# GpSimd makes layer A's mask and query latents earlier, VectorE adds eps and evicts early products ahead of its weight chunks

## The reference

```
layer A:  x += tanh(g) * xattn_A(LN(x), LN(context), mask)   8 heads of 64; kv = context and gated latents
          x += tanh(g) * moe(LN(x))                          8 experts, top 2 per token, width 512
layer B:  x += tanh(g) * xattn_B(LN(x), LN(context), mask)   16 heads of 64
          x += tanh(g) * ffn_B(LN(x))                        rows and weights quantised, 256 -> 1024,
                                                             depthwise conv of 3, activation, 1024 -> 256
LN(v) = (v - mean) * rsqrt(var + 1e-5) * gamma + beta
xattn: softmax(q k^T + mask) v, then an output projection; keys are 112 latents and 375 context rows
```

## Time and profile before

| | |
|---|---|
| median of 3 runs | 1506.27 us (1496.41 to 1508.53) |
| profiled execution | 1507.64 us, its span 1505.9 us |
| granted TensorE clock, mean | 0.935 |
| busy: TensorE, VectorE, ScalarE, GpSimd | 83%, 71%, 65%, 74% of the span |
| DMA engines | 239.94 MB, mean 159 GB/s |

### The profile page before, as it was taken

How to read it: one execution, slowest core, us unless ns; L and a number is a source line. 1 busy time by engine, 2 the same in 40 slices (tenths; PEclk the granted TensorE clock), 3 DMA queues, 4 the chain that set the end, 5 groups by cost and what they waited for, 6 DMA issues and landing times.

```text
span 1505.9 us, 44898 instructions
## 1 busy us (share of the span) xinstructions
PE 1252.2 (83%) x16822; PEld 980.5 (65%) x16822; DVE 1075.0 (71%) x2786; ACT 973.2 (65%) x2319; POOL 1116.6 (74%) x1359
## 2 busy tenths in 40 slices
PE   1868787768769898977999999899999999999842
PEld 0545565547658776655887887677777777777631
DVE  4868786876555556775666766688888888888744
ACT  2868785555545576654655555687888887787731
POOL 5869787686566675547676777789889888988754
PEclk9989998889999999987999999999999999999965
DMA  7499999886999974547999999544655455454520
GB/s 223 98 232 229 230 241 221 166 219 148 242 179 249 235 171 91 93 101 181 236 229 252 247 256 241 107 106 97 104 97 105 104 108 104 95 110 102 78 41 6
DMA packets 439336, 239.94 MB, mean 159 GB/s; under 512 B 388960, under 2 KB 420560, under 8 KB 430544
## 3 DMA queue, kind: packets, MB, share of 16 engines
q1 hardware_dynamic: 407496, 172.87, 56.6%
q10 hardware_dynamic: 28552, 56.86, 12.4%
q0 software_dynamic: 3072, 7.34, 1.8%
HBM read 107.78 MB, written 35.50 MB: 95 GB/s over the span
## 4 chain that ended last, share of the span: by engine, by line
PE 32%; POOL 23%; DMA 13%; DVE 10%; issue 7%; ACT 6%; SPq 4%; DVEq 2%; ACTq 1%; POOLq 0%
PE bank_ring L1089 6%; DMA probs_turned<-probs 6%; POOL probs L651 6%; DMA expert_up<-experts_up 6%; PE bank_ring L1075 5%; PE bank_ring L1127 5%; PE bank_scores L1049 4%; PE bank_out L1108 3%; POOL raw_weights L696 3%; PE bank_x L1188 2%; ACT scores L852 2%; PE bank_x L1141 2%; POOL raw_weights L697 2%; POOL affine L627 2%; SPq L521 2%
## 5 line engine op out<-in xcount | busy, mean ns | idle before, releaser
L651 POOL TENSOR_TENSOR probs<-scores,probs 112x487 f16<-112x487 f32 x384 | 425.9, 1126 | 223.1 <-ACT probs L859 218.3
L852 ACT ACTIVATE scores<-scores,score_min 112x487 f32<-112x487 f32 x384 | 265.5, 693 | 81.8 <-DVE score_min L1340 79.5
L1340 DVE CUSTOM_DVE_ANT_0 scores<-bank_scores,mask 112x487 f32<-112x487 f32 x384 | 239.1, 660 | 48.9 <-PE bank_scores L1049 43.8
L859 ACT ACTIVATE probs<-scores 112x487 f16<-112x487 f32 x384 | 214.7, 604 | 37.0 <-DMA probs_turned<-probs 21.8
L1089 PE MATMUL bank_ring<-weights,kv_B 128*128 128x128 f16 x3072 | 196.8, 222 | 1.8 <-DVE keys L1352 1.8
L1089 PEld LDWEIGHTS bank_ring<-weights,kv_B 128*128 128x128 f16 x3072 | 185.8, 99 | 11.1 <-DVE keys L1352 2.5
L1108 PE MATMUL bank_out<-values,probs_turned 128*128 128x64 f16 x4608 | 171.3, 194 | 23.3 <-DMA probs_turned<-probs 22.7
L1357 DVE SCALAR_TENSOR_TENSOR values<-bank_ring,values 128x512 f16<-128x512 f32 x192 | 131.2, 683 | 80.4 <-ACT values L879 80.4
L879 ACT ACTIVATE values<-bank_ring 128x512 f16<-128x512 f32 x192 | 112.6, 587 | 110.5 <-PE bank_out L1108 109.1
L1075 PE MATMUL bank_ring<-kv_B,weights 128*128 128x488 f16 x768 | 181.1, 372 | 0.0
L1108 PEld LDWEIGHTS bank_out<-values,probs_turned 128*128 128x128 f16 x4608 | 158.6, 99 | 26.7 <-DMA probs_turned<-probs 13.0
(11 more groups left out here) (230 smaller groups left out, 2474.8 us busy)
## 6 DMA issues: line engine op xcount, KB each, us to landing
expert_up<-experts_up SPq DMA_DIRECT2D x43, 1024.0 KB, 5.3
expert_down<-experts_down SPq DMA_DIRECT2D x43, 512.0 KB, 6.8
raw_weights<-in_weights ACTq DMA_DIRECT2D x8, 1536.0 KB, 11.1
experts_up<-expert_up ACTq DMA_DIRECT2D x8, 1024.0 KB, 4.8
raw_weights<-in_weights ACTq DMA_DIRECT2D x6, 1024.0 KB, 8.3
probs_turned<-probs SPq DMA_TRANSPOSE x384, 3.3
context_turned_B<-kv_B ACTq DMA_DIRECT2D x16, 375.0 KB, 9.1
kv_B<-context_turned_B ACTq DMA_DIRECT2D x16, 375.0 KB, 3.7
```

The lines of the kernel that those rows point to most:

```text
L651: pool.tensor_tensor(PR[:, u % 4, 1, 0:KEYS], S[:, u % 4, 0:KEYS], PR[:, u % 4, 0, 0:KEYS], ALU.subtract).then_inc(probs_split, 1)
L852: act_e.activation(S[:, u % 4, 0:KEYS], S[:, u % 4, 0:KEYS], ACT.Exp, bias=rmin[:, u % 4:u % 4 + 1], scale=-1.0, accum_out=rsum[:, g % 2, ...
L859: act_e.activation(PR[:, u % 4, 0, 0:KEYS], S[:, u % 4, 0:KEYS], ACT.Copy).then_inc(probs_ready, 1)
L1340: dve.tensor_tensor_reduce(out=S[:, u % 4, 0:KEYS], in0=bS[u % 2][0:TOK, 0:KEYS], in1=mask[:, m, 0:KEYS], scale=1.0, scalar=3.0e38, op0=AL ...
```

## The change

Five edits:

1. GpSimd's `split_latents` is cut in three. `split_query_latents(n)` runs at step 4n-5, after that step's split_context of layer B and ahead of its split_probs. `make_mask(0, n)` runs at step 4n-4, ahead of split_context. What is left at step 4n-3 is the gated latents alone, and they raise `kv_ready`. Sequence 0 keeps one block in step -5, in the new order. Layer B's `split_latents` still makes its mask.
2. ScalarE's `round_latents` is cut likewise: the query latents' high part at step 4n-5, ahead of `round_context`; the gated ones stay at step 4n-4.
3. SP loads layer A's mask bytes at step 4n-6 instead of 4n-5, waiting for `mask_made` instead of `kv_ready`.
4. The multiplication and addition of eps in `rstd` move to VectorE: a drain and one `tensor_scalar` after each `bn_aggr`, two for P. GpSimd keeps the power.
5. On VectorE the early evictions (and `gate_hidden`) stand ahead of `split_expert` and `quantise_ffn_weights`. `split_l1_chunk` stays ahead of `gate_hidden` in steps with an expert tile, and comes after the evictions in others.

```diff
             def load_mask(layer, n):
-                sp.wait_ge(kv_ready[layer if n else 0], n if n or not layer else NSEQ)
+                if layer == 0:
+                    sp.wait_ge(mask_made, n)
+                else:
+                    sp.wait_ge(kv_ready[layer if n else 0], n if n else NSEQ)
...
-                if (j - 3) % 4 == 0 and 0 < (j + 5) // 4 < NSEQ:
-                    load_mask(0, (j + 5) // 4)
+                if (j - 2) % 4 == 0 and 0 < (j + 6) // 4 < NSEQ:
+                    load_mask(0, (j + 6) // 4)
...
             def rstd(stage, n, cols):
-                m, r = mv[stage], rs[stage]
+                r = rs[stage]
                 pool.wait_ge(stats_ready[stage], n + 1)
-                after(pool.tensor_tensor(r[:, 0:cols], m[:, 0:cols, 1], growth[:, 0:cols], ALU.mult))
-                after(pool.tensor_tensor(r[:, 0:cols], r[:, 0:cols], bias[:, 0:cols], ALU.add))
                 pool.tensor_tensor(r[:, 0:cols], r[:, 0:cols], minus_half[:, 0:cols], ALU.pow)\
                     .then_inc(rstd_ready[stage], 1)
...
+            def split_query_latents(n):
+                pool.wait_ge(x1_drained, X1_AT[("p_lat", n)])
+                for kb in range(KB):
+                    scale, shift = latent_vec(V_GLAT, kb)
+                    last = pool.tensor_scalar(affl[:, 0, kb], latT[:, kb], scale, shift, ALU.mult, ALU.add)
                 after(last)
+                pool.wait_ge(latq_hi, n + 1)
+                after(pool.tensor_tensor(latq[:, n % 2, :, 1], affl[:, 0], latq[:, n % 2, :, 0], ALU.subtract))
+
+            def make_mask(layer, n):
                 a, b = (MASKED, 0.0) if layer == 0 else (-MASKED, MASKED)
...
+                return pool.tensor_scalar(mask[:, n % 2, TOK:KEYS], mask8[:], a, b, ALU.mult, ALU.add)
+
+            def split_latents(layer, n):
+                c = 8 + V_GLAT if layer else V_GATED
...
+                pool.wait_ge(lat_hi[layer], n + 1)
+                last = pool.tensor_tensor(lo, affl[:, 0], hi, ALU.subtract)
+                if layer:
+                    after(last)
+                    last = make_mask(layer, n)
+                last.then_inc(kv_ready[layer], 1)
+                if layer == 0:
+                    pool.wait_ge(kv_ready[0], n + 1)
...
                 if (j + 4) % 4 == 0 and 0 < (j + 4) // 4 < NSEQ:
+                    make_mask(0, (j + 4) // 4).then_inc(mask_made, 1)
                     split_context((j + 4) // 4, 0, 0)
...
+                if (j + 5) % 4 == 0 and 0 < (j + 5) // 4 < NSEQ:
+                    split_query_latents((j + 5) // 4)
...
                 if (j + 5) % 4 == 0 and 0 <= (j + 5) // 4 < NSEQ:
-                    round_context((j + 5) // 4)
+                    n = (j + 5) // 4
+                    round_latents(n, latq[:, n % 2], V_GLAT, latq_hi)
+                    round_context(n)
                 if (j + 4) % 4 == 0 and 0 <= (j + 4) // 4 < NSEQ:
-                    round_latents((j + 4) // 4)
+                    n = (j + 4) // 4
+                    round_latents(n, kv[0][:, n % 2, :, :, 0:TOK], V_GATED, lat_hi[0])
...
                 dve.drain()
-                dve.bn_aggr(mv[stage][0:TOK, 0, :], bn[0:TOK, at, :]).then_inc(stats_ready[stage], 1)
+                dve.bn_aggr(mv[stage][0:TOK, 0, :], bn[0:TOK, at, :])
+                dve.drain()
+                dve.tensor_scalar(rs[stage][0:TOK, 0:1], mv[stage][0:TOK, 0, 1:2], 1.0 + LN_EPS, LN_EPS * LN_EPS,
+                                  ALU.mult, ALU.add).then_inc(stats_ready[stage], 1)
...
+                if m[0]:
+                    for c in l1_chunk(j - 1):
+                        split_l1_chunk(c)
+                    gate_hidden(m[0][1], m[0][2], m[0][3])
+                for t in early(j):
+                    part(t)
                 for c in expert_chunks(j - 1):
                     split_expert(c)
                 quantise_ffn_weights(j)
-                for c in l1_chunk(j - 1):
-                    split_l1_chunk(c)
-                if m[0]:
-                    gate_hidden(m[0][1], m[0][2], m[0][3])
-                for t in early(j):
-                    part(t)
+                if not m[0]:
+                    for c in l1_chunk(j - 1):
+                        split_l1_chunk(c)
```

56 lines of the change are left out of this document (24 added, 32 removed).

## The result

The changed kernel takes 1534.68 us, the median of four runs (1526.26 to 1536.71), against 1506.47 before: ratio 1.0221, 95% interval 1.0169 to 1.0273. It is 28 us slower. A run over 1.5% above its kernel's fastest is left out of every ratio in this text. The profiled execution took 1536.71 us, its span 1535.0, 29.1 more than before's.

A forecast was written before the change was run, and what follows sets the result against it. No engine was taken to bound the whole: the chain lies on TensorE 32%, GpSimd 23%, DMA 13%. Terms -0.3 -1.2 -6.5 +1.7 -4 +1.5 -3.5 -1 sum to -13.3: 1493 us against 1506.3, range 1472 to 1511.

The forecast's parts named there:

- one added wait is within 0.1: GpSimd's run ahead of a sequence's first query product: 2.0 of 3.6 us leave, and the added wait costs within 0.1.
- The slower rival: Query latents ahead of split_probs delay transposes 1.6 to 2.2 us, behind bursts, 11 us more each: 1526 us, chance 12%.
- Step 2: TensorE's 3.6 us wait for GpSimd's mask at the first query product shrinks: -1.2 us, bounds 0 and 2.0.
- A wait removed just ahead of such a stretch is only paid later: 65 to 268 us: a 14.74 us transpose follows; three of six mask waits count as followed by one, three as free.
- 65 to 268 us: Layer A: -3.3 us from six waits for GpSimd's mask and -3.2 from VectorE's early evictions, together -6.5.
- The scatter: Around 341 us: the last scatter, behind more GpSimd work, delays the first expert product: +1.7 us, bounds 0 and 2.2.
- 380 to 554 us: TensorE's 26.0 us of waits for expert_up shrink as SP issues these loads sooner: -4 us, bounds 0 and 9.
- eps: Less GpSimd work in rstd, more on VectorE: layer B -3.5 us, tail -1, start -0.3, layer A +1.5.
- VectorE's order: 65 to 268 us: early products evicted ahead of weight chunks, some keys 1.28 us late: -3.2 us, between -6 and +6.
- the third stretch above: 780 to 955 us: TensorE busy 166.68 of 175 us, DMA share 1.01 at 239 GB/s; the change can do nothing.
- The last sign named: Forecast wrong if probabilities' transposes newly queue behind bursts, or DMA share falls well below 0.98 while both stretches shrink 20 us.

The follow-up runs named there:

- queries_behind_probs: The changed kernel with GpSimd's query latents of step 4n-5 behind both split_probs of that step instead of ahead of them: ratio 1.0139 to the kernel before.
- rounding_ahead: The changed kernel with ScalarE's rounding of the query latents ahead of its rounding of the probabilities in step 4n-5, not at the step's end: ratio 1.0100.
- act_round_early: The kernel before with only ScalarE's rounding of the query latents moved a step earlier, GpSimd and SP keeping their order: ratio 1.0084.
- after_l1_late: The changed kernel with ScalarE's first load of layer B's raw weights, 1 MB, at step 39 instead of 37: ratio 1.0165 to the kernel before.
- the main pair: The kernel before, 1506.47 us, and the changed kernel with all five edits, 1534.68 us: ratio 1.0221.
- the light pair: The kernel before and the changed kernel, each with five sixths of the experts' raw loads left out: 1488.9 us (0.9916) and 1512.1 us (1.0103).
- eps_only: The kernel before with only the multiplication and addition of eps moved to VectorE: ratio 1.0055.
- order_only: The kernel before with only VectorE's early evictions moved ahead of its weight chunks: ratio 0.9980.
- no_latents: The changed kernel without the moves of mask, query latents and mask load, so only eps on VectorE and VectorE's new order: ratio 1.0003.
- spread_l1_late: The kernel before with experts' raw loads in three smaller DMAs each and layer B's first raw-weight load at step 39 instead of 37: ratio 0.9935.
- mask_early: The kernel before with the mask made at step 4n-4 on GpSimd and its bytes loaded at 4n-6 on SP, all latents staying: ratio 1.0011.

## Why the prediction was wrong

*The step that failed* is in the part on GpSimd: "one added wait is within 0.1". The handshake was priced, not the place of its partner. The prediction knew that GpSimd would wait for ScalarE ("ahead of its exponentials, and GpSimd waits for these"), but the rounding stands at the end of its step, ahead of the next step's exponentials and behind both roundings of the probabilities of its own. The waits were 94.7 us in 15 times, 6.3 each, 47.6 us more in all than GpSimd waited for ScalarE before, and behind each are queued two split_probs, two transposes on SP and ScalarE's rounding four heads on, which needs the buffer. Without the wait the loss is 0.8 to 1.2% smaller (queries_behind_probs, rounding_ahead). Nothing in the trace of before showed this wait, but both orders did. A second term was left out, as if it cost nothing: ScalarE's rounding a step earlier, which alone costs 0.8% (act_round_early); why it does stays open.

*The slower rival* had the family right: query latents ahead of split_probs, transposes issued late and behind bursts, 1526 us. It was priced by 1.6 to 2.2 us of work per sequence, which rounding_ahead shows not to be the main part, and given 12%. In step 7 the delay was 5.75 us. So it was near the result, 1534.7, partly by luck. Its 11 us for each transpose were taken against a median of 3.3 us over the whole run, and from 50 to 300 us the median before is 6.3. The range was also narrower than the chances: it ended at 1511 with 8% above, while this rival at 1526 had 12%.

*Step 2* (-1.2): the wait at the query product fell from 3.6 to 2.0 us, but behind it came one of 6.7 us for a transpose:

```profile
PE bank_out L1123 <- DMA probs_turned<-probs: 6.7, 1, 6.7
PE bank_x L1077 <- POOL kv_A L643: 2.0, 1, 2.0
```

The transpose at 50.84 was 0.5 us ahead of the spill and took 11.5 us; before it was 1.25 ahead and landed in 6.1. The step took 4.1 us more. "A wait removed just ahead of such a stretch is only paid later" held here, with interest. How much is chance: in the profile of after_l1_late, the same program up to step 36, this wait is 2.7 us.

*65 to 268 us* (-6.5) measured plus 18. Its parts were near: the waits for GpSimd fell by 11.1 of at most 12, those for VectorE's evictions by 3.5 of at most 6, and five keys were to come late by 1.28; they did so six times, 6.1 us. What was missing in this profile is 11.7 us more for transposes and 6.3 us more of busy TensorE. The forecast let the DMAs absorb no more than the gain; they can take more. In the profile of after_l1_late the wait for transposes in these steps is only 20.1 us, and the stretch is still 10.9 us longer than before's.

*The scatter* (+1.7) was right where it was priced: the first expert product starts 16.2 us after the step's start before (325.5 to 341.75) and 17.9 after (353.1 to 371.04). Its wait is 6.62 us, for which "some 10" was expected. The step is 3.9 us longer, since behind it TensorE waits 1.9 us for the keys. What was not seen is the jump that lies beside it, some 6 or some 10 us from scatter to load; in both profiles of the main pair it is the long one, in the light pair it is 5 of the 11.2 us that the changed kernel loses in the step.

*380 to 554 us* (-4) gave nothing: TensorE waits 28.8 us in twelve times (380 to 632) where it waited 26.0 in five (350 to 600), and some 20 were expected.

```profile
PE bank_ring L1142 <- DMA expert_up<-experts_up: 28.8, 12, 8.9
```

Steps 43 and 47 are 1.9 and 5.0 us shorter, steps 51, 53 and 55 together 3.9 longer. What was not seen is step 59, 3.2 us longer: VectorE waits 8.46 us there for the gathered rows of the mixture's result, and TensorE 9.1 us for VectorE's queries behind them (before 7.00 and 6.6).

*eps.* Layer B: forecast -3.5 (2.7 to 5.0 less). TensorE's waits from 985 to 1469 us (for the earlier trace rows):

```profile
PE bank_x L1249 <- DVE raw_weights L1601: 7.9, 9, 1.1
PE bank_x L1253 <- DVE raw_weights L1610: 6.0, 10, 0.6
```

Nine waits of 0.9 us and the second group up, as forecast, and it is edit 4 that does it: the first group is 7.8 us in eps_only and stays 12.7 in order_only. The two groups together are 2.8 us less. But the time hardly shows it: from step 104 to 191 the changed kernel takes 492.3 us, eps_only 492.5 and order_only, without eps, 492.8, against 493.0 before, and all profiles lie between 491.4 and 494.0. Of the 6 us that come back after step 60, 5 lie between steps 60 and 104, 3.6 of them from step 80, about the stretch of which the prediction said that the change can do nothing; from 60 to 104 order_only gains 3.7, no_latents 2.0, eps_only 1.9. In layer A +1.5 was too little: eps_only as a whole is 0.55% slower, some 8 us, and its one profile, at 1503.9 us of span, doesn't show where. That stays open.

*VectorE's order* (-3.2) has the size of order_only's 0.998, or 3 us, but that is luck as far as the runs tell: the interval reaches from 8 us faster to 2 slower, and in the stretch for which it was forecast order_only's profile is 10.4 us longer (208.6 against 198.2 from step 5 to 31). The Trainium skill's figure, 341 GB/s for transfers of 1 MB ("DMA: Bandwidth & Descriptors", Bandwidth), was weighed against rows and left; the third stretch above again shows only 242 GB/s at share 0.98.

*The last sign named*, that the forecast is wrong "if the probabilities' transposes queue behind bursts where they didn't", is what the trace of the changed kernel shows in step 2, and the wait for turned probabilities grew past 18.7 us, to 30.4.

## What to carry to other kernels

When an instruction moves ahead on one engine, look up where its partner stands in the other engine's order, not only what the handshake costs: a producer at the end of the same step turned a 0.6 us subtraction into a 6 us stall for everything queued behind. Put such a consumer behind the step's critical hand-overs, or the producer ahead of them. And where stretches run with full DMA queues, an issue that slips past another engine's burst can change price in a jump (from 6 to 10 us here), so look at the order of issue between queues, not only at microseconds. Last, take a second profile of the same program before a single step is explained: here one step took 8.6 us in one and 16.2 in the other.

## What the runs showed of the hardware

- TensorE's busy time for the same products varies with the granted clock, and not with the loss: from step 5 to 31 it is 152 us at 0.91 before, 159 at 0.89 in the changed kernel, but 159 at 0.89 in order_only too, which is as fast as before. In the changed kernel's step 10, with two long waits, the clock was 0.76.
- When ScalarE's 1 MB load was issued 3.4 to 3.6 us ahead of the last scatter of rows, these rows could be read 8.2 to 12.1 us after the scatter's issue (nine profiles); when it was issued at most 2.5 us ahead or behind it, 5.4 to 6.7 us (nine profiles). With the load away it was 6.3 us in the changed kernel and 2.8 in spread_l1_late.
- The same program varied by 3.6% between runs (1476 to 1529 us, over several chips), and a single profile can lie 12 us from its kernel's median (mask_early: 1495.9 against 1507.7). Over the same instructions, steps 5 to 31, two profiles differed by 7.6 us (216.7 and 209.1).
